# Six small edits around the gated-linear-attention loop of a two-layer decoder kernel

## The reference

```python
x = x + _L0_attn_ref(_layernorm(x), Wq, Wk, Wv, Wg, gk_w1, gk_w2, gk_b, Wo, rms_w)

def _L0_attn_ref(x, ...):
    q = (x @ Wq) * 32 ** -0.5 ; k = x @ Wk ; v = x @ Wv        # per head
    g = log_sigmoid(x @ gk_w1 @ gk_w2 + gk_b) / 16
    # scan over time, per head:  S = exp(g_t)[:, None] * S + k_t v_t^T ;  o_t = q_t @ S
    o = o * rsqrt(mean(o * o, axis=-1) + 1e-5) * rms_w         # per head, 64 channels
    return (o.reshape(b, t, 256) * silu(x @ Wg)) @ Wo
```

## Time and profile before

| | us |
|---|---|
| median of 3 runs (486.99 to 487.4) | 487.13 |
| the profiled execution's own time | 486.1 |
| its span | 484.2 |
| PE busy in it | 436.4 |
| DVE busy in it | 367.5 |
| ACT busy in it | 282.6 |
| mean granted TensorE clock | 0.972 |

### The profile page before, as it was taken

How to read it: one execution, slowest core, us unless ns; L and a number is a source line. 1 busy time by engine, 2 the same in 40 slices (tenths; PEclk the granted TensorE clock), 3 DMA queues, 4 the chain that set the end, 5 groups by cost and what they waited for, 6 DMA issues and landing times.

```text
span 484.2 us, 12911 instructions
## 1 busy us (share of the span) xinstructions
PE 436.4 (90%) x4480; PEld 306.3 (63%) x4480; DVE 367.5 (76%) x989; ACT 282.6 (58%) x615; POOL 210.1 (43%) x543
## 2 busy tenths in 40 slices
PE   3879878987879999699999999999999997999897
PEld 1335565655865778456767666676666765887656
DVE  3767948998778898977877877777787867566666
ACT  2762324655438787386777777777777766413460
POOL 5050011281021557126666667576666676342200
PEclk9999968999887999999999999999999999999999
DMA  6399932710000130000000000000000000000001
GB/s 214 67 98 100 100 34 71 246 36 1 0 1 14 45 108 18 17 1 18 3 19 1 3 16 0 16 0 0 0 0 0 0 1 1 3 2 1 0 2 43
DMA packets 15620, 15.78 MB, mean 33 GB/s; under 512 B 1348, under 2 KB 12859, under 8 KB 15579
## 3 DMA queue, kind: packets, MB, share of 16 engines
q1 hardware_dynamic: 15579, 15.24, 15.3%
HBM read 10.52 MB, written 4.72 MB: 31 GB/s over the span
## 4 chain that ended last, share of the span: by engine, by line
PE 71%; DVE 20%; ACT 4%; issue 3%; DMA 1%; POOL 0%; SPq 0%; DVEq 0%; ACTq 0%; POOLq 0%
PE bank L928 16%; PE bank L1430 11%; PE bank L1382 9%; PE bank L1305 5%; PE bank L1213 4%; PE bank L1226 3%; PE bank L1423 3%; PE bank L1301 3%; PE bank L1320 2%; DVE PX L1731 2%; DVE mx L1729 2%; PE bank L1542 1%; PE bank L1038 1%; PE bank L1550 1%; DVE Y L1580 1%
## 5 line engine op out<-in xcount | busy, mean ns | idle before, releaser
L832 ACT ACTIVATE SN<-SN,nmx 128x512 f32<-128x512 f32 x128 | 92.7, 725 | 9.4 <-DVE nmx L1943 6.9
L928 PE MATMUL bank<-cs,SN 128*128 128x128 f32 x512 | 67.3, 274 | 3.8 <-DVE Z L1936 1.6
L928 PEld LDWEIGHTS bank<-cs,SN 128*128 128x128 f32 x512 | 57.2, 141 | 18.6 <-issue 12.5
L1382 PE MATMUL bank<-TK,TQ 64*128 64x512 f16 x384 | 52.6, 379 | 1.6 <-DVE TK L1906 1.6
L542 POOL TENSOR_TENSOR CTW<-YT 128x128 f32<-128x128 f32 x64 | 29.6, 463 | 52.1 <-DVE YT L1941 51.4
L1928 DVE CUSTOM_DVE_ANT_0 SN<-bank,strip 128x512 f32<-128x512 f32 x64 | 43.3, 677 | 1.2 <-PE bank L1382 0.6
L1943 DVE CUSTOM_DVE_ANT_0 SN<-bank,strip 128x512 f32<-128x512 f32 x64 | 43.6, 681 | 0.0
L1936 DVE COPY PTO<-bank 128x512 f32<-128x512 f32 x32 | 22.1, 692 | 20.4 <-PE bank L1430 19.0
L1936 DVE COPY Z<-bank 128x512 f32<-128x512 f32 x32 | 22.1, 691 | 17.0 <-PE bank L1430 15.5
L843 ACT COPY PTO<-bank 128x512 f32<-128x512 f32 x32 | 18.7, 586 | 26.4 <-PE bank L1430 26.4
L1430 PE MATMUL bank<-Z,TV 128*64 128x128 f32 x512 | 33.4, 273 | 0.0
(11 more groups left out here) (316 smaller groups left out, 981.5 us busy)
## 6 DMA issues: line engine op xcount, KB each, us to landing
bias_rows<-biasr SPq DMA_DIRECT2D x1, 4096.0 KB, 44.4
band<-bias_rows SPq DMA_DIRECT2D x1, 3072.0 KB, 12.4
wqkv<-in_twqkv SPq DMA_DIRECT2D x8, 192.0 KB, 2.7
w1s<-in_w SPq DMA_DIRECT2D x8, 128.0 KB, 2.0
w2s<-in_w SPq DMA_DIRECT2D x8, 128.0 KB, 2.3
wB<-in_wb SPq DMA_DIRECT2D x1, 753.0 KB, 5.9
wA<-in_wa SPq DMA_DIRECT2D x1, 520.0 KB, 4.9
X<-in_x SPq DMA_DIRECT2D x2, 256.0 KB, 3.3
```

The costliest lines, as they stand in the source:

```text
L832: sc.activation(p, p, ACT.Exp, bias=nmx[:, r % RING, h:h + 1], scale=-1.0, accum_out=psm[:, r % RING, h:h + 1]).then_inc(sm["exp_ready"], 1)
L928: return nc.tensor.transpose(out_, in_, ident[0:n, 0:n])
L1382: ins = mm(bank[2 * (s % 2) + h][:, :], TQ[u][r, q_part, S * b + P * qt:S * b + P * qt + P], TK[u][r, k_part, S * b:S * b + S], start=(k = ...
```

## The change

Six edits, all in the first block:

1. POOL writes the tile `ones` first of all, and PE begins with 15 products of it.
2. Of the four copies of `QX` for batch 0, ACT keeps two and POOL takes two.
3. PE turns over only batch 0's `KP` ahead of the loop; that of batch 1 (`keys_t(1)`) stands in the loop after `gla_o(0)`. On DVE the making of batch 1's `KP` (`keys_out(1)`) stands after `gla_mask(0)`.
4. On ACT both value copies of tiles 0 and 1 come before the load of the Silu table, the two gates after it; the semaphore `vg_ready` is counted twice per tile, so that PE can wait for the values alone (`values_at`) or for the gate too (`gate_at`).
5. `gla_vg(t)` stands at the end of a tile, two tiles ahead; before, it stood after `gla_kv`, three tiles ahead.
6. The squares are taken head by head with the sum as accumulator output (four instructions of 64 columns for one of 256); `head_sums` on DVE is gone.

```diff
@@ gpsimd
+            gp.memset(ones[:, :], 1.0).then_inc(sm["konst_ready"], 1)
...
-            gp.memset(ones[:, :], 1.0).then_inc(sm["konst_ready"], 1)
...
+            pool.wait_ge(sm["ow_ready"], 1)
+            pool.wait_ge(sm["qs_ready"], 1)
+            for h in range(GH // 2, GH):
+                r = slice(GK * h, GK * h + GK)
+                if h == GH - 1:
+                    pool.wait_ge(sm["qx_pool"], 1)
+                gp.tensor_copy(QX[r, 0:TG, h, :], QS[r, 0:S].rearrange("p (t c) -> p t c", c=P)).then_inc(sm["qx_ready" if h == GH - 1 else "qx_pool"], 1)
@@ scalar
-            for h in range(GH):
+            for h in range(GH // 2):
                 r = slice(GK * h, GK * h + GK)
                 sc.copy(QX[r, 0:TG, h, :], QS[r, 0:S].rearrange("p (t c) -> p t c", c=P)).then_inc(sm["qx_ready"], 1)
...
+            take_keys(0)
+            for t in range(2):
+                take_values(t)
+            act.preload_act_table_set("silu_and_others")
+            for t in range(2):
+                take_gate(t)
+            take_keys(1)
 
             def take_o(t):
                 act.wait_ge(sm["o_mm"], t + 1)
-                sc.activation(SQ[:, t, :], bank[4 + t % 2][:, 0:DV], ACT.Square).then_inc(sm["sq_ready"], 1)
-
-            for t in range(NT):
+                for h in range(GH):
+                    d = slice(GV * h, GV * h + GV)
+                    ins = sc.activation(SQ[:, t, d], bank[4 + t % 2][:, d], ACT.Square, accum_out=SS[:, GH * t + h:GH * t + h + 1])
+                ins.then_inc(sm["sq_ready"], 1)
+
+            for t in range(2, NT):
                 if t >= 3:
                     take_o(t - 3)
...
@@ tensor
+            pe.wait_ge(sm["konst_ready"], 1)
+            keep_busy(5, 15)
             pe.wait_ge(sm["ld_cs"], 16)
             norm_t(0, 0, Y)
...
-            for g in range(NG):
-                keep_busy(5, 4)
-                pe.wait_ge(sm["kp_ready"], g + 1)
+
+            def keys_t(g):
+                pe.wait_ge(sm["kp_ready"], 2 * g + 1)
                 for t in range(TG):
                     ins = tr(bank[4 + g][:, P * t:P * t + P], KP[:, S * g + P * t:S * g + P * t + P])
                 ins.then_inc(sm["kp_tp"], 1)
+            keep_busy(5, 4)
+            keys_t(0)
...
-                pe.wait_ge(sm["qx_ready"], GH * (i // TG + 1))
-                pe.wait_ge(sm["kp_ready"], 2)
+                pe.wait_ge(sm["qx_ready"], GH * (i // TG + 1) - 1)
+                pe.wait_ge(sm["kp_ready"], min(i, 1) + 1)
...
                 pe.wait_ge(sm["kpt_ready"], i // TG + 1)
-                pe.wait_ge(sm["vg_ready"], i + 1)
+                pe.wait_ge(sm["kp_ready"], 2)
+                pe.wait_ge(sm["vg_ready"], values_at(i))
...
             gla_a(0)
-            gla_vg(2)
             for i in range(NT):
                 gla_kv(i)
-                if i + 3 < NT:
-                    gla_vg(i + 3)
                 if i + 1 < NT:
                     gla_a(i + 1)
...
                 gla_o(i)
+                if i == 0:
+                    keys_t(1)
+                if i + 2 < NT:
+                    gla_vg(i + 2)
@@ vector
+            def keys_out(g):
+                vv.tensor_tensor(KP..., KC..., ed, ALU.mult).then_inc(sm["kp_ready"], 1)
...
+                if g == 0:
+                    keys_out(0)
+                else:
+                    ins.then_inc(sm["kp_ready"], 1)
...
-            def head_sums(g):
-                dve.wait_ge(sm["sq_ready"], TG * g + TG)
...
             gla_mask(0)
+            keys_out(1)
...
-                if i == TG:
-                    head_sums(0)
...
             norm_rows(1, 0, X, Y)
-            head_sums(1)
             gate_out(NT - 1)
```

More of the change, by code:

```diff
@@ L310, in build @@
         HT = sb("HT", [P, FB, TOK])
-        names = """ld_x ld_cs ld_a ld_b ld_c ld_d bias_dma dve_c act_c qx_ready konst_ready
+        names = """ld_x ld_cs ld_a ld_b ld_c ld_d bias_dma dve_c act_c qx_ready qx_pool konst_ready
             ln_var ln_rstd ln_y ln_tp ln_yt x_done
             qk_mm h1_mm h1_ready gl_mm u_ready l_ready g_ready e_ready kp_ready qs_ready kp_tp kpt_ready vg_mm vg_ready
-            a_mm am_ready kv_mm st_ready o_mm ob_ready sq_ready ss_ready sr_ready og_ready ot_mm ot_ready go_mm
+            a_mm am_ready kv_mm st_ready o_mm ob_ready sq_ready sr_ready og_ready ot_mm ot_ready go_mm
             kv_x_mm kb_ready kx_ready vx_ready vs_mm vb_ready qt_mm qt_hi qt_ready xb_ready s_mm px_sub px_ready pt_mm pt_ready xo_mm ct_ready ws_ready co_mm
@@ L397, in _ @@
             gp.memset(reset[:, :], 1.0).then_inc(sm["konst_ready"], 1)
-            pool.wait_ge(sm["konst_ready"], 3)
+            pool.wait_ge(sm["konst_ready"], 4)
             gp.memset(reset[:, :].rearrange("p (c s) -> p c s", s=CH)[:, :, 0:1], 0.0).then_inc(sm["konst_ready"], 1)
@@ L417, in _ @@
                 r = slice(GK * h, GK * h + GK)
-                pool.wait_ge(sm["qx_ready"], GH + h)
+                pool.wait_ge(sm["qx_ready"], GH - 1 + h)
                 gp.tensor_copy(QX[r, TG:NT, h, :], QS[r, S:TOK].rearrange("p (t c) -> p t c", c=P)).then_inc(sm["qx_ready"], 1)
-            pool.wait_ge(sm["qx_ready"], 2 * GH)
+            pool.wait_ge(sm["qx_ready"], 2 * GH - 1)
             def expand_keys(part):
@@ L628, in _ @@
             act.preload_act_table_set("natural_log_exp_and_others")
-            act.wait_ge(sm["konst_ready"], 2)
+            act.wait_ge(sm["konst_ready"], 3)
             for g in range(NG):
@@ L659, in _, with take_keys, take_values, take_gate @@
             act.wait_ge(sm["qs_ready"], 1)
-            for h in range(GH):
+            for h in range(GH // 2):
                 r = slice(GK * h, GK * h + GK)
                 sc.copy(QX[r, 0:TG, h, :], QS[r, 0:S].rearrange("p (t c) -> p t c", c=P)).then_inc(sm["qx_ready"], 1)
-            for g in range(NG):
+            def take_keys(g):
                 act.wait_ge(sm["kp_tp"], g + 1)
                 sc.copy(KPT[:, TG * g:TG * g + TG, :], bank[4 + g][:, :].rearrange("p (t c) -> p t c", c=P)).then_inc(sm["kpt_ready"], 1)
-                if g == 0:
-                    act.preload_act_table_set("silu_and_others")
+            def take_values(t):
+                act.wait_ge(sm["vg_mm"], t + 1)
+                sc.copy(V[:, t, :], bank[6 + t % 2][:, 0:DV]).then_inc(sm["vg_ready"], 1)
+            def take_gate(t):
+                sc.activation(SG[:, t, :], bank[6 + t % 2][:, DV:2 * DV], ACT.Silu).then_inc(sm["vg_ready"], 1)
+            take_keys(0)
[5 more added lines that the diff above has]
+            take_keys(1)
             def take_o(t):
                 act.wait_ge(sm["o_mm"], t + 1)
-                sc.activation(SQ[:, t, :], bank[4 + t % 2][:, 0:DV], ACT.Square).then_inc(sm["sq_ready"], 1)
-            for t in range(NT):
+                for h in range(GH):
[3 more added lines that the diff above has]
+            for t in range(2, NT):
                 if t >= 3:
                     take_o(t - 3)
-                act.wait_ge(sm["vg_mm"], t + 1)
-                sc.copy(V[:, t, :], bank[6 + t % 2][:, 0:DV])
-                sc.activation(SG[:, t, :], bank[6 + t % 2][:, DV:2 * DV], ACT.Silu).then_inc(sm["vg_ready"], 1)
+                take_values(t)
+                take_gate(t)
             act.preload_act_table_set("natural_log_exp_and_others")
@@ L683, in rms_of @@
                 c = slice(TG * GH * g, TG * GH * (g + 1))
-                act.wait_ge(sm["ss_ready"], g + 1)
+                act.wait_ge(sm["sq_ready"], TG * g + TG)
                 link(sc.activation(SL[:, c], SS[:, c], ACT.Ln, bias=eps, scale=1 / GV))
@@ L1016, in gla_o @@
             def gla_o(i):
-                pe.wait_ge(sm["kpt_ready"], 2)
+                pe.wait_ge(sm["kpt_ready"], min(i, 1) + 1)
                 pe.wait_ge(sm["am_ready"], i + 1)
@@ L1035, in gla_vg @@
             def gla_vg(t):
-                pe.wait_ge(sm["vg_ready"], t - 1)
+                pe.wait_ge(sm["vg_ready"], gate_at(t - 2))
                 mm(bank[6 + t % 2][:, :], YT[:, P * t:P * t + P], wA_("vg", 2 * DV), start=True, stop=True).then_inc(sm["vg_mm"], 1)
@@ L1042, in gla_t @@
                 pe.wait_ge(sm["og_ready"], g + 1)
+                pe.wait_ge(sm["vg_ready"], gate_at(NT - 1))
                 for half in range(2):
@@ L1623, in _ @@
                 vv.tensor_tensor(GC[:, c].rearrange("p (k s) -> p k s", s=CH), g3, mid.to_broadcast([P, CB, CH]), ALU.subtract).then_inc(sm["g_ready"], 1)
+            def keys_out(g):
+                c = slice(S * g, S * g + S)
+                ed = ED[:, CB * g:CB * g + CB].rearrange("p (k o) -> p k o", o=1).to_broadcast([P, CB, CH])
+                vv.tensor_tensor(KP[:, c].rearrange("p (k s) -> p k s", s=CH), KC[:, c].rearrange("p (k s) -> p k s", s=CH), ed,
+                                 ALU.mult).then_inc(sm["kp_ready"], 1)
             for g in range(NG):
@@ L1629, in _ @@
                 link(vv.tensor_tensor(KC[:, c], bank[2 + g][:, :], E2[:, c], ALU.mult))
```

(10 more changed lines are left out.)

## The result

The changed kernel takes 480.43 us (median of 4 runs, 476.99 to 482.53), the kernel before 487.06 beside it: ratio 0.9859, 95% interval 0.9821 to 0.9898. With six more runs of it the median of all ten is 480.0. It scatters by 6.5 us from run to run. Ratios and intervals leave out runs that lie over 1.5% above the fastest of their kernel; where a median changes by that, both are given. The profiled execution took 480.13, with a span of 478.3.

What follows compares the result with a forecast made beforehand. PE, DVE and ACT alternate in the front, PE binds the loop, DVE the last tiles. Terms 0.92 + 3.35 - 1.15 + 0.3 - 0.4 = 3.0 take 487.13 to 484.1 us; range 481.0 to 486.4.

Steps and rivals of the forecast that it cites:

- the front: Kernel start: products of ones raise PE's clock early; turns end 0.41 earlier, the product pair saves 0.51, sum 0.92 us.
- the rest of the block: Block behind the front: loop start 3.35, loop -1.15, end of loop 0.3, tail -0.4 us.
- Start of the loop: First tiles: gla_kv(0) waits for the last QP, and gla_kv(1) starts at 31.55 instead of 34.92, gain 3.35 us.
- Loop: Between gla_kv(1) and gla_kv(6): five value products instead of four, tiles 3.89 apart, leaving 2.2 of the 3.35 us.
- Squares, end, tail: Last tiles and behind: squares 1.2 us per tile on ACT, first half's turn 2.5 earlier, next Y 0.4 later.
- The 0.4 lost in the tail: Behind the product with Wo: four squares make the root ready at 3.3, not 2.6, so the next Y comes 0.4 later.
- Copies on POOL: POOL copying beside DVE's KC, QP and mask: slowdown taken as 0, upper bound 1.3 us in all.
- The rival with the kinder clock: Behind the edits, one slow-clock stretch costing 3.0 us goes, giving 481.1 us; chance 0.13.

Runs made afterwards that it cites:

- filled pair: Kernel before and changed kernel, each with unread products of ones in all four PE pauses of the block: 482.01 and 475.70 us.
- the products alone: Kernel before plus only the tile of ones written first and the 15 products at the start: 484.42 us, ratio 0.9959.
- filled, without them: Changed kernel with all four PE pauses filled with unread products, but without the 15 products at the start: 478.04 us.
- filled with the sums on DVE: Changed kernel with all four PE pauses filled, one Square per tile and the sums of squares back on DVE: 476.16 us.
- loop's start filled: Changed kernel plus 5 unread products ahead of the first turn of the keys and 2 ahead of the loop: 479.44 us.
- both turns first: Changed kernel with both turns of the keys ahead of the loop again: 482.85 us.
- all copies on ACT: Changed kernel with all four copies of batch 0's QX on ACT again: 484.23 us, or 481.81 without five slow runs.
- sums on DVE: Changed kernel with one Square of 256 columns per tile and the sums of squares back on DVE: 481.29 us.
- filled kernel before: Kernel before with unread products added in the same four PE pauses and no ones at the start: 482.01 us.

## Why the prediction was wrong

Its sign and most mechanisms held; its size did not. The two terms that were too small are the front (0.92, where the medians give 1.9 to 2.4) and the rest of the block (2.1, where the traces give 2.9). In the filled pair, 5.0 to 6.3 us apart, are placed: the start 1.9 (`U` at 14.79, the median of the seven traces without the ones, against 12.9) and the other edits 2.9.

**Front.** "0.92 ... more can't be had" is the first failed step, in two ways. It was too small even for the execution that I read: against it `U` came 1.26 earlier (12.79 for 14.05). The turns ended 0.50 earlier, where 0.41 was forecast, and the pair took 1.82 in place of 2.57, where I had 2 x 1.03 = 2.06: the second matmul's 1.03 was not what this product takes at the full level. And that execution had an early rise of the clock. In the traces without the ones `U` came at 13.80, 13.89, 14.05, 14.79, 15.03, 15.09 and 15.16, with them at 12.8 to 13.0 each time. The gain is 0.8 to 2.4 by run. The medians say 2.3 on one chip (the products alone, against the kernel before), 1.9 on another (filled, without them, against filled with the sums on DVE), and 2.4 and 2.3 between chips. The 15 products themselves cost nothing, as booked: they ran from 0.99 to 6.7 us, and the first `Y` came behind 8. One trace can't show the spread of a clock that rises at its own moment.

**Start of the loop.** The order of waits was right: `gla_kv(0)` waits for `QP`, nothing else is late. At the full clock `gla_kv(1)` stands at 30.21 (loop's start filled) against 34.85 - 1.22 = 33.63 (the start's saving in these two traces): 3.42, forecast 3.35. What I did not see is that PE, busy for 1.37 of 3.5 us ahead of it, can then get the low clock for the first tile. It did in both traces of the changed kernel, where it cost about 3 us, and in two of the variants (both turns first, all copies on ACT). It did not in two others with the same pauses (no products at the start, sums on DVE), and in none of the seven traces of the changed kernel's variants with the loop's start filled. So the fall goes with the pauses, but it doesn't come in each execution, and six traces don't tell how often it does.

**Loop.** Of 3.42 were left 2.4 at `gla_kv(6)` (49.64 against 53.23 - 1.22 = 52.01); forecast 2.2.

**Squares, end, tail.** These terms were mis-sized: 0.79 for 1.2. The turn of the first half waited for DVE and not for ACT: in the changed kernel's trace tile 5's last square is over at 56.05, while DVE was at its masks until 56.25, where the forecast had DVE free and waiting for the squares. The turn came 2.9 earlier beyond the start's saving (54.83 against 58.94 - 1.22), forecast 2.5. The 0.4 lost in the tail was not lost. Together 0.8: the block's 2.1 became 2.9.

**Copies on POOL.** Zero was right: `QP` took 0.70 and `KC` 0.61 on the chain beside POOL's copies.

**The clock behind.** The rival with the kinder clock (481.1) gave nearly the measured time, but that is luck in the main: with the low clock filled away in the block the edits still give 5.0 to 6.3. Filling took 4.9 us off the kernel before and 4.3 to 4.7 off the changed one, so the low clock costs both about the same. In the one profiled pair a part did go as that rival has it (the 1.2 us of the experts' first products), but not in the changed kernel's second trace.

**Left open.** Of the filled pair's 5.0 to 6.3, 0.2 to 1.5 are neither in the start nor in the block. In the second layer's attention the first and the last `TQ` on DVE (L1906 in the kernel before) start 193.6 us apart or more in each trace of the kernel before, filled or not, and 193.2 in each of the changed one and its variants; that is 0.4 and has no explanation here. Another 0.3 lies outside the span (2.1 us in the median for the filled kernel before, 1.8 for the changed one). The remainder, up to 0.8, is within what medians from different chips can tell.

## What to carry to other kernels

Before costing an edit at the head of a kernel or around a pause of PE, read the granted clock and the doubled durations in more than one execution: one trace shows one moment of the clock's rise or fall, and the median moves by the average over them. An edit that shortens a chain can leave PE with a thinner stretch, and in some executions the low clock then takes back what was won; unread products in the pauses held it up in this block in every trace, and the median fell by 4.3 us. And compare variants with the pauses filled, and on one chip: the scatter fell from 6.5 us (ten runs) to 1.2 (five), while the same path took 475.7 on one chip and 476.2 on another.

## What the runs showed of the hardware

The same program, on the same data, has its clock changes at different places from run to run: low from 26 to 32.4 and from 67 to 73.4 us in one trace of the changed kernel, from 27 to 33, 57 to 64 and 71 to 74 in another. A stretch in which PE was busy for 1.34 to 1.37 of 3.5 us was followed by the low level in these two traces, and by the full level in that with the sums on DVE. At the start the profile's granted clock reads 1.00 although the first products run at the low speed; only the durations (3.60 against 2.48 for the same four records) tell.

DVE instructions with two SBUF inputs lengthen beside POOL. The state update takes 0.48 us in the other tiles; in the first tile of the changed kernel, beside POOL's `KX`, it took 0.97:

```profile
28.06 1.22 POOL L434 TENSOR_TENSOR KX<-KB,inside 128x616 f16<-128x616 f32 x1
...
28.59 0.97 DVE L1701 SCALAR_TENSOR_TENSOR ST<-ST,E,KVM 128x256 f32<-128x256 f32 x1
```

That is the rule of the Trainium skill (GPSIMD Engine Reference, Specifications) on two SBUF inputs, and the trace agrees: `KC` and `QP`, with one input in PSUM, took 0.67 and 0.69 beside POOL's copies (0.68 and 0.69 in the kernel before, without them), and `KP`, with both inputs in SBUF, took 1.10 there for 0.68.
